# A graph network's second attention layer: the order of mask loads and transposes on one DMA queue

## The reference

```python
q = (x @ Wq + bq).reshape(n, H, C)
k = (x @ Wk + bk).reshape(n, H, C)
v = (x @ Wv + bv).reshape(n, H, C)
alpha = jnp.einsum('ehc,ehc->eh', q[dst], k[src]) / jnp.sqrt(jnp.float32(C))
...
p = jnp.exp(alpha - amax[dst])
denom = jax.ops.segment_sum(p, dst, num_segments=n) + 1e-16
out = jax.ops.segment_sum(p[:, :, None] * v[src], dst, num_segments=n)
out = out / denom[:, :, None]
out = out.reshape(n, H * C) if concat else out.mean(axis=1)
return out + x @ Ws + bs
...
h = jax.nn.relu(transformer_conv(x, ..., H1, C1, True))
out = transformer_conv(h, ..., H2, C2, False)
...
x = _layernorm(x + out, axis=-1)
```

## Time and profile before

| | |
|---|---|
| median of 3 runs | 1829.64 us (1829.35 to 1830.43) |
| the profiled execution | 1829.15 us, span of its instructions 1827.3 us |
| busy: PE, DVE, ACT, POOL | 1732.7, 1555.2, 1259.5, 1169.5 us |
| PE in 1520 to 1560 us, inside layer 2 | 40.00 of 40.00 us busy |
| granted TensorE clock, mean | 0.982 of full speed |

### The profile page before, as it was taken

The page is one execution under the profiler, slowest core; times in us unless marked ns, Lnnn a source line. Parts: engine busy times, 40 slices in busy tenths (PEclk is TensorE's granted clock), DMA queues, the critical chain, the costliest instruction groups (busy, mean ns, idle before and its releaser), DMA issues. The chain is left out here.

```text
span 1827.3 us, 45046 instructions
## 1 busy us (share of the span) xinstructions
PE 1732.7 (95%) x15000; PEld 1301.8 (71%) x15000; DVE 1555.2 (85%) x4541; ACT 1259.5 (69%) x2093; POOL 1169.5 (64%) x1461
## 2 busy tenths in 40 slices
PE   3779799999999999999999999989899999999997
PEld 2556567777777777777777777756677777677775
DVE  7999888988888898888888888835788888988886
ACT  4579877777777777777777777732566676666675
POOL 4200057787877777777767777733577777777776
PEclk9899999999999999999999999999999999999999
DMA  6779857777778777778777887692599999989995
GB/s 163 227 201 259 236 120 158 156 154 154 154 159 161 159 156 153 155 164 157 159 153 153 161 162 155 127 233 54 106 174 185 174 185 177 172 176 184 172 188 108
DMA packets 753664, 301.76 MB, mean 165 GB/s; under 512 B 655863, under 2 KB 734075, under 8 KB 750184
## 3 DMA queue, kind: packets, MB, share of 16 engines
q1 hardware_dynamic: 752266, 296.96, 78.2%
q0 software_dynamic: 640, 1.63, 0.3%
q10 hardware_dynamic: 528, 0.26, 0.0%
HBM read 93.63 MB, written 47.83 MB: 77 GB/s over the span
## 5 line engine op out<-in xcount | busy, mean ns | idle before, releaser
L1429 POOL TENSOR_TENSOR prob_parts_l<-prob_l,prob_parts_l 125x512 f16<-125x512 f32 x600 | 720.5, 1231 | 13.6 <-ACT prob_parts_l L1544 13.6
L1535 ACT ACTIVATE prob_l<-prob_l,neg_max_l 125x1024 f32<-125x1024 f32 (+1 forms) x450 | 521.2, 1160 | 2.1 <-DVE neg_max_l L1630 1.8
L1836 PE MATMUL score_l<-room,QT_l 128*128 128x512 f16 (+2 forms) x2100 | 512.7, 354 | 1.4 <-DVE scale_rows L1802 1.2
L1550 ACT CAST probT_l<-transposed_l 128x375 f16<-128x375 f32 x450 | 213.0, 473 | 410.0 <-PE transposed_l L1862 410.0
L1877 PE MATMUL output_l<-V,prob_flipped_l 128*128 128x256 f16 x2400 | 459.6, 272 | 1.3 <-DMA prob_flipped_l<-prob_parts_l 1.3
L1879 PE MATMUL output_l<-V,prob_flipped_l 128*128 128x128 f16 x2400 | 427.5, 219 | 0.0
L1622 DVE CUSTOM_DVE_ANT_0 prob_l<-score_l,mask_even 125x512 f32<-125x512 f32 (+2 forms) x546 | 332.7, 614 | 85.8 <-PE score_l L1836 84.2
L1622 DVE CUSTOM_DVE_ANT_0 prob_l<-score_l,mask_odd 125x512 f32<-125x512 f32 (+2 forms) x504 | 307.9, 614 | 78.0 <-PE score_l L1836 76.3
L1544 ACT CAST prob_parts_l<-prob_l 125x1024 f16<-125x1024 f32 x300 | 309.4, 1033 | 0.1
L1877 PE MATMUL output_l<-V,probT_l 128*128 128x256 f16 x1350 | 272.0, 273 | 2.7 <-DVE probT_l L1635 1.9
L1877 PEld LDWEIGHTS output_l<-V,prob_flipped_l 128*128 128x128 f16 x2400 | 233.7, 97 | 52.2 <-issue 1.9
(11 more groups left out here) (217 smaller groups left out, 2375.4 us busy)
## 6 DMA issues: line engine op xcount, KB each, us to landing
mask_scratch<-log SPq DMA_DIRECT2D x87, 420.0 KB
mask_even<-mask_scratch SPq DMA_DIRECT2D x25, 448.0 KB
mask_odd<-mask_scratch SPq DMA_DIRECT2D x24, 448.0 KB
mask_odd<-mask_scratch SPq DMA_DIRECT2D x12, 896.0 KB
mask_even<-mask_scratch SPq DMA_DIRECT2D x12, 896.0 KB
prob_flipped_l<-prob_parts_l SPq DMA_TRANSPOSE x600, 3.1
hT_scratch<-rowsT_l SPq DMA_DIRECT2D x24, 250.0 KB, 3.6
mask_odd<-mask_scratch SPq DMA_DIRECT2D x12, 471.2 KB
```

The lines of the kernel that those rows point to most:

```text
L1429: pool.tensor_tensor(parts[0:TP, 1, a:b], prob[:, h % 2, a:b], parts[0:TP, 0, a:b], ALU.subtract).then_inc(s_flo, 1)
L1535: act.activation(e, e, ACT.Exp, bias=neg_max[:, h % 2:h % 2 + 1], accum_out=total[:, h % 2, c:c + 1]).then_inc(s_exp, 1)
L1550: act.copy(probT[:, q, 0, 0:n, 0:TP], flipped_in_psum(h, q, n)).then_inc(s_hi, 1)
L1836: last = pe.matmul(score_bank(h, p)[:, 0:b - a], QT[:, h % 2, i, :], KT[:, h, j, a:b], start=n == 0, stop=n == len(PRODUCTS) - 1)
```

## The change

In layer 2, SP issues a step's four transposes first and the step's load of mask rows behind them. In layer 1 the order stays.

```diff
                             for rows_ab in STORES_AT.get((t, h), ()):
                                 store_rows(*rows_ab)
+                        tn, hn = ahead(t, h, 1)
+                        if layer == 2 and exists(tn):
+                            flips(s + 1, hn)
                         n, j = divmod(h + 2, H)
                         if not (n == 0 and is_first(t)) and exists(t + 1 + n):
                             if j == 0:
                                 sp.wait_ge(s_masked, NP * H * (t + n))
                             load_mask(t + 1 + n, (parity + 1 + n) % 2, j)
-                        tn, hn = ahead(t, h, 1)
-                        if exists(tn):
+                        if layer == 1 and exists(tn):
                             flips(s + 1, hn)
```

## The result

The change makes the kernel slower: 2034.41 us (2029.93 to 2038.70, 4 runs) against 1829.49 (1827.92 to 1830.43), a ratio of 1.111 with a 95% interval of 1.110 to 1.113. The profiled execution took 2038.70 us with a span of 2036.6, 209.3 us more than that of before. Over the 23 loads of a first part that is 9.1 us each (8.9 by the medians); I had forecast 6.8.

The account below looks back on a forecast made before the run. PE was taken to bound layer 2. A tile of 10.81 + 6.5 + 9.12, plus 1.0 for the clock, is 27.43 us against 20.65; 23 x 6.78 = 156 on 1829 gives 1985 us, range 1938 to 2042.

Parts of the forecast that it names:

- What bounds it: Layer 2: PE sets the pace, busy 20.80 of 20.80 us over one tile, so sooner transfers earn nothing.
- The transposes cannot be hurried: SP, layer 2: they wait for ACT and POOL data, so the first part is issued 10.81 us behind the maximum.
- The landing: First mask-row part, issue to landing: 6.5 us, ends 6.3 (quickest similar load) and 8.1; at most 9.70 from the trace.
- From DVE's work to the maximum: Last loop stretch, DVE's first work on the new part to next-but-one `neg_max`: 9.12 us plus 1.0 for the clock.
- DVE's ready pieces: Three score pieces ready after the stall give DVE 2 to 3 us of work, covering half the clock's 1.9 us.
- The 9.12 for full clock: DVE's first work to `neg_max` without clock loss: 1.82, 5.64 and 1.66 us, 9.12 in all.
- It returns every tile: Layer 2 loop: load issue hangs on the maximum and the maximum on the last load, so the wait recurs each tile.
- Paid once: Rival: the loop is broken and the stall comes once, 6.8 us, giving 1836 us; chance 0.04.
- The second part costs nothing: Second mask-row part, 526 KB, moves likewise but the step with the first part's stall covers it: 16.8 us against 15 to 16.
- The transposes: High-part transposes land in 3.0 us, not up to 8.1, but PE never waited for them, so this earns nothing.
- The sum: 23 first-part loads times 6.78 us a tile, 156 us, added to 1829 gives 1985 us, 8.5% slower.
- The dearer rival: Landing takes 8.1 us and DVE covers no clock loss: 9.28 more a tile, 213 in all, 2042 us; chance 0.12.

Follow-up runs that it names:

- PE kept busy: Full change, with PE given 30 matmuls on a tile of zeros once a tile during its stall: 1992.55 us, 1.088 against the kernel before.
- the run behind two transposes: Against the kernel before, both mask-row parts are issued between the two high and two low transposes of their step: 1896.06 us.
- the late-work run: Full change, with DVE's work on newly loaded rows put later in its program: 1885.91 us, 1.030 against the kernel before; same late work with old order 1854.50.

## Why the prediction was right, and where it was short

- **What bounds it.** Right: PE had no wait to lose, so nothing could be gained, and the loss came as a new wait of DVE's that PE could not cover. The stall of PE stands where I put it, at the product behind that `low_part`; it is 7.0 us where I said some 5.
- **The transposes cannot be hurried.** Right: they took 7.17 us on SP before and after the earlier trace rows, and start 3.93 behind the maximum. The issue came 11.14 behind the maximum, against 10.81 forecast. The 0.33 is ACT's: its exponentials start 0.52 behind the maximum, no longer 0.19, since its cast of PE's last transposed blocks (1547.06, after 0.50 of waiting for PE) now comes in between. That PE is late there because of its stall is inferred.
- **The landing**, 6.5 forecast, is 7.36 in the tile shown and 7.20 in the median. This term was mis-sized. The nearest row, 6.3, was too low an anchor, as the quickest of its kind; the right lean was towards the middle of the bounds. The estimate by the Trainium skill's page "DMA: Bandwidth & Descriptors" (section "Anatomy of one DMA — SWDGE (gpsimd) path"), 4.35, is further off; its rate is for DMAs from GpSimd, and these come from SP. No run issues this load from another engine, so what makes the difference is not shown.
- **From DVE's work to the maximum**, 10.12 forecast with the clock, is 11.02 in that tile. Here a step failed: that DVE's ready pieces would cover half of the clock's loss. The 9.12 for full clock was right (9.20 with PE kept busy). The table shows a loss of 1.9 to 2.0 us a tile besides the wait, the whole 1.9 that the earlier trace rows give for one spell. DVE does use its ready pieces, but then waits for PE's scores, so they buy nothing:

```profile
1541.83 0.69 DVE L1624 CUSTOM_DVE_ANT_0 prob_l<-score_l,mask_even 125x512 f32<-125x512 f32 x1 [1.18 <-PE score_l L1838]
...
1543.39 0.56 DVE L1624 CUSTOM_DVE_ANT_0 prob_l<-score_l,mask_even 125x384 f32<-125x384 f32 x1 [0.85 <-PE score_l L1838]
```

The Trainium skill's page "TensorE: Matmul & The Clock Gate" (section "HAM oscillation — how this bites in real kernels") tells of a loop whose DMA wait sends the array to its lower clock in every turn; the change does so here (0.50 in the stretch behind the stall shown, a mean of 0.85 from 1400 to 1700 us), and the run behind two transposes, with 2.45 us of wait a tile and a mean clock of 0.979, does not.
- **It returns every tile.** Right: 23 waits for 23 loads. Paid once is out.
- **The second part costs nothing.** Right in the full change (no wait but the 23), and the reason holds: alone it costs 180 us, together with the first nothing. In the late-work run, where the first part's stall is gone, it is the second part that DVE waits for.
- **The transposes** earn nothing by going first. Right: PE waited for one once, 0.5 us, in all of layer 2 before.
- **The sum.** 0.33 + 0.86 + 0.90 = 2.1 us a tile on my 6.78 give 8.87 (29.52 - 20.65), and 23 times that is 204 us. That one tile fits the 205 so closely is partly luck: over 22 turns the loop takes 29.94 us in the mean against 20.92 before, 9.0 more. The tile is off by more than the 1.5 us that I had set as the sign of a mis-sized landing or clock, and both were. The dearer rival (2042 us) came nearest in time: its clock was right, its landing of 8.1 too long. The measured 2034 stands 49 us over the central 1985 and within 8 of the range's upper end, so the range was reached with some luck: what that rival has too much in the landing makes up for what its other terms lack.

## What to carry to other kernels

On a queue that is issued in order, a load that is moved behind other transfers inherits their waits, not only their bytes: look at what the last of them waits for and add it to the load's landing before asking whether the load has time. If the buffer's user also feeds the work that lets the next load go, the lateness is a loop and is paid in every turn. When two moves each lie on a loop of their own, undoing one shows little gain (here none for the second part and 23 of the 205 us for the first); only the longer loop sets the time.

## What was not expected

- The first work on new rows is slow in the change: 0.83 and 1.11 us in the rows above, where 0.68 was usual for 512 columns. It is not that the load has just woken DVE. In the run behind two transposes all 23 woken works take 0.69 to 0.76, and in the kernel before a work that waited for nothing takes 1.43. The slow ones run beside POOL's subtractions. Behind two transposes, DVE and then POOL:

```profile
1551.71 0.69 DVE L1612 SCALAR_TENSOR_TENSOR mask_even<-mask_even 125x512 f32<-125x512 f32 x1 [2.77 <-DMA mask_even<-mask_scratch]
```

```profile
1553.52 5.41 POOL L1433 TENSOR_TENSOR prob_parts_l<-prob_l,prob_parts_l 125x512 f16<-125x512 f32 x4 [0.34 <-DMA prob_flipped_l<-prob_parts_l]
```

In the change, POOL beside the 1.11 of 1565.41; in the kernel before, DVE's slow work and the subtractions beside it:

```profile
1562.60 4.93 POOL L1431 TENSOR_TENSOR prob_parts_l<-prob_l,prob_parts_l 125x512 f16<-125x512 f32 x4
```

```profile
1549.48 1.43 DVE L1608 SCALAR_TENSOR_TENSOR mask_odd<-mask_odd 125x512 f32<-125x512 f32 x1
```

```profile
1548.09 4.96 POOL L1429 TENSOR_TENSOR prob_parts_l<-prob_l,prob_parts_l 125x512 f16<-125x512 f32 x4
```

In layer 2 of the kernel before, every work on 512 columns without a subtraction beside it takes 0.68 to 0.70 us (68 of them); the 24 beside one take 1.43 in the median. No run moves the subtractions alone, so the two go together in the traces, but no edit tests it.
- Matmuls on zeros, 30 in each stall, made a kernel faster by 42 us. It remains 8.8% slower than before; no run points to a version that beats the kernel before.
